# Attention of 2048 queries: V products and row sums of two steps put together, with six slots of probabilities, a K ring of six and a Q ring of three

## The reference, cut to what matters

```python
q, k, v = jnp.split(qkv, 3, axis=-1)
scores = jnp.einsum('bhqd,bhkd->bhqk', q, k) / np.sqrt(HEAD_DIM)
causal = jnp.tril(jnp.ones((S, S), dtype=bool))[None, None]
scores = jnp.where(causal, scores, NEG)
probs = jax.nn.softmax(scores, axis=-1)
ctx = jnp.einsum('bhqk,bhkd->bhqd', probs, v)
return ctx.transpose(0, 2, 1, 3).reshape(B, S, DIM) @ W_out + b_out
```

## Time and profile before

| | |
|---|---|
| median of 3 runs | 2070.89 us (2069.48 to 2071.95) |
| time of the profiled execution | 2070.12 us, its span 2067.9 us |
| PE busy over the span | 1959.5 us (95%) |
| DVE busy | 1076.5 us (52%) |
| ACT busy | 638.3 us (31%) |
| POOL busy | 454.2 us (22%) |
| mean granted clock of TensorE | 0.983 |

### The profile page before, as it was taken

The page is one execution under the profiler, slowest core; times in us unless marked ns, Lnnn a source line. Parts: engine busy times, 40 slices in busy tenths (PEclk is TensorE's granted clock), DMA queues, the critical chain, the costliest instruction groups (busy, mean ns, idle before and its releaser), DMA issues. The chain is left out here.

```text
span 2067.9 us, 25594 instructions
## 1 busy us (share of the span) xinstructions
PE 1959.5 (95%) x10088; PEld 1398.7 (68%) x10088; DVE 1076.5 (52%) x1860; ACT 638.3 (31%) x1152; POOL 454.2 (22%) x401
## 2 busy tenths in 40 slices
PE   6999999999999997889999999997998979999998
PEld 4677555445555545678888888885885668888886
DVE  4456877667666725743434443436434575434334
ACT  3231355446455563422112111113221332111111
POOL 0122766666645266100000000000002110000000
PEclk9999999999999999999999999999999999999999
DMA  8653421422421003200000000002001011000002
GB/s 311 224 161 124 93 52 43 93 53 53 97 46 27 20 1 133 67 31 31 30 2 31 31 31 1 1 1 90 6 6 31 0 41 41 24 28 21 5 1 82
DMA packets 61720, 111.86 MB, mean 54 GB/s; under 512 B 6000, under 2 KB 21248, under 8 KB 61568
## 3 DMA queue, kind: packets, MB, share of 16 engines
q1 hardware_dynamic: 54144, 85.05, 14.3%
q0 software_dynamic: 7456, 25.18, 4.1%
HBM read 84.77 MB, written 25.44 MB: 53 GB/s over the span
## 5 line engine op out<-in xcount | busy, mean ns | idle before, releaser
L450 DVE TENSOR_REDUCE part_max<-banks 128x1 f32<-128x512 f32 (+2 forms) x640 | 357.5, 615 | 154.7 <-PE banks L422 95.0
L921 ACT ACTIVATE probs<-banks 128x512 f32<-128x512 f32 (+3 forms) x640 | 310.7, 538 | 281.1 <-PE banks L848 141.1
L422 PE MATMUL banks<-kst,qst 96*128 96x512 f32 (+2 forms) x640 | 261.4, 417 | 12.9 <-DVE part_max L450 9.2
L844 PE MATMUL banks<-qst,kst 98*128 98x512 f32 (+2 forms) x640 | 250.8, 412 | 0.2 <-ACT probs L921 0.2
L1423 DVE TENSOR_TENSOR tokens_a<-banks,tokens_a 128x512 f32<-128x512 f32 x224 | 151.6, 688 | 69.6 <-PE banks L214 68.9
L212 PE MATMUL banks<-h_hi,f_w_first 128*128 128x512 f32 x448 | 177.3, 396 | 9.5 <-DVE h_lo L199 9.5
L1448 DVE TENSOR_TENSOR tokens_b<-banks,tokens_b 128x512 f32<-128x512 f32 x64 | 44.3, 692 | 270.0 <-ACT tokens_b L1367 270.0
L213 PE MATMUL banks<-h_lo,f_w_first 128*128 128x512 f32 x448 | 176.9, 395 | 0.0
L212 PE MATMUL banks<-f_d_hi,f_hid_hi 128*128 128x512 f32 x432 | 170.0, 393 | 6.7 <-issue 3.6
L214 PE MATMUL banks<-h_hi,f_w_first 128*128 128x512 f32 x448 | 176.3, 393 | 0.0
L213 PE MATMUL banks<-f_d_lo,f_hid_hi 128*128 128x512 f32 x432 | 168.2, 389 | 0.0
(11 more groups left out here) (187 smaller groups left out, 3251.8 us busy)
## 6 DMA issues: line engine op xcount, KB each, us to landing
tokens_a<-in_L_wmod SPq DMA_DIRECT2D x12, 1024.0 KB, 7.9
qst<-q_hi SPq DMA_DIRECT2D x32, 256.0 KB, 6.1
kst<-k_hi SPq DMA_DIRECT2D x32, 256.0 KB, 8.2
x<-in_L_attn_x SPq DMA_DIRECT2D x4, 1024.0 KB, 12.9
q_hi<-qk_out_hi POOLq DMA_DIRECT2D x16, 256.0 KB, 3.0
q_lo<-qk_out_lo POOLq DMA_DIRECT2D x16, 256.0 KB, 3.3
k_hi<-qk_out_hi POOLq DMA_DIRECT2D x16, 256.0 KB, 4.2
k_lo<-qk_out_lo POOLq DMA_DIRECT2D x16, 256.0 KB, 4.3
```

The lines of the kernel that those rows point to most:

```text
L422: mm = nc.tensor.matmul(dst[:, 0:wide], qst[n % QS][0:BIASROW, h, P * t:P * t + P], kst[(NB * g + c) % KS][0:BIASROW, h, 0:wide], start=Tr ...
L450: nc.vector.tensor_reduce(part_max[:, n % 2, ht, c:c + 1], max_bank(slot)[:, 0:wide], AX_X, ALU.max).then_inc(max_read, 1)
L844: mm = nc.tensor.matmul(dst[:, c0:512], kst[ck % KS][0:BIASROW + 2, h, at:at + P], qst[n % QS][0:BIASROW + 2, h, c0:512], start=True, stop ...
L921: nc.scalar.activation(probs[:, q % PS, h, c0:512], score_bank(sh)[:, c0:512], ACT.Exp, scale=SCALE).then_inc(exp_done, 1)
```

## The change

The middle is done once for two steps. Steps s and s+1 (s even, always of one block) form a pair, and TensorE's order is: both quads of step s; then one middle with `sum_pair(s-3)`, `context(s-2)`, `context(s-1)` and `sum_pair(s-2)`; then both quads of step s+1. Probabilities have six slots, because they live longer. To pay for the two slots in SBUF, Q has three buffers instead of four and K six instead of seven. So `load(3)` moves from the start of the attention to the end of block 0's scores, and every later `load(n)` waits for block n-3 instead of n-4; `schedule()` uses the same QS, so its limits move too. For n = 6, 7, 10, 11, 14 and 15 the turn of block n-1 now stands ahead of the first tile of block n. `finalize` moves from the second quad of a block's first step to the first quad of its second step, and waits for `pairs_used` too. The waits of ACT on GpSimd's pair sums go back three steps instead of two.

```diff
-            QS = 4
-            KS = 7
-            PS = 4
+            QS = 3
+            KS = 6
+            PS = 6
...
-                    if n and i == TURN_AFTER:
+                    if n and i == (0 if n % NB in (2, 3) and n > QS else TURN_AFTER):
                         slots.append((n - 1, tiles_of(n - 1)))
...
-                for n in range(3):
+                for n in range(QS):
                     load(n)
                 rows_of_max(0)
-                load(3)
...
                 def sum_pair(s):
                     n, i = steps[s]
+                    if not off_diagonal(s):
+                        return
...
-                for s, (n, i) in enumerate(steps):
+                for s in range(0, len(steps), 2):
                     phase(s, 0)
-                    if s >= 2 and off_diagonal(s - 2):
+                    phase(s, 1)
+                    if s:
+                        if s >= 4:
+                            sum_pair(s - 3)
+                        context(s - 2)
+                        context(s - 1)
                         sum_pair(s - 2)
-                    if s:
-                        context(s - 1)
-                    phase(s, 1)
+                    phase(s + 1, 0)
+                    phase(s + 1, 1)
+                sum_pair(len(steps) - 3)
+                context(len(steps) - 2)
                 context(len(steps) - 1)
...
-                            if q >= PS and off_diagonal(s - 2):
-                                act.wait_ge(pair_ready, 4 * off_index(s - 2) + h + 1)
+                            if q >= PS and off_diagonal(s - 3):
+                                act.wait_ge(pair_ready, 4 * off_index(s - 3) + h + 1)
...
                     if part == 0:
                         dve.wait_ge(probs_read, quads_before(n + 1))
+                        if j:
+                            dve.wait_ge(pairs_used, off_before(n + 1))
...
-                    for slot in max_of_quad[2 * s]:
-                        max_vector(dve, slot)
-                    tiles = max_of_quad[2 * s + 1]
+                    tiles = max_of_quad[2 * s]
                     for part in range(4):
-                        if n and i == 0:
+                        if n and i == 1:
                             finalize(n - 1, part)
                         for slot in tiles[len(tiles) * part // 4:len(tiles) * (part + 1) // 4]:
                             max_vector(dve, slot)
+                    for slot in max_of_quad[2 * s + 1]:
+                        max_vector(dve, slot)
```

## The result

The changed kernel takes **2172.97 us** (2171.31 to 2182.06, four runs) against 2070.18 us before: a ratio of 1.051, 95% interval 1.048 to 1.054, or 103 us more. The direction was forecast, the size wasn't: 2127 us was, with a range that ends at 2158.

A forecast was written before the change was run, and what follows sets the result against it. TensorE was taken to bound the attention, busy 567 of 581 us. Merge -14.4, slots +58, turns +1.5, loads +5 and clock +6 gave +56 us on 2070.9: 2127 us, range 2095 to 2158.

The forecast's parts named there:

- The bursts: Crowded quads with 17, 16 and 16 slots, where VectorE sets the pace: 12.2 us lost three times, 36 us.
- about 5.5: Sign in the attention: 40 middles of about 5.5 us instead of 80 of 2.9.
- 80 us or more: Sign in the attention: TensorE's wait for VectorE's reductions grows from 45 us to 80 or more.
- part 5: Half-clock windows where VectorE is full; middles falling into them take 1.7 us more: +6 us (0 to 35).
- third rival: TensorE stays at 1.2 GHz for most of the bursts, 16 us each, 48 in three: 2169 us, chance 0.10.
- Part 4: Turns right behind their block's last tile, +1.5 us (0 to 5); late Q and K loads, +5 (0 to 24).
- Parts 1 and 2: Merging 80 middles into 40 saves 14.4 us; four quads between middles lengthen stretches set by the slowest engine.
- The rule of three instructions' head start: Stretch between middles takes the longer of TensorE's sum and the slowest engine's quad-by-quad sum less 1.5 us.
- droughts: Quads without maximum tiles, where ScalarE needs 2.0 us against TensorE's 0.94: 9 us in the three groups.
- part 3: Three Q buffers change the slots in each quad: 78 us lost less 20 lost before, +58 us.
- the switch wins: The 40 saved middles, 14.4 us, outweigh VectorE's lag: 2056 us, chance 0.04.
- The middle rival: Crowded quads cost only themselves: 36 us, 6 for empty quads, -14 for merging: 2098 us, chance 0.16.

The follow-up runs named there:

- e5: Kernel before, with its buffers and single middles, given the changed kernel's slots in each quad and places of the turns: 2149.27 us.
- e1: Changed kernel with one middle in each step and finalize in its old place, keeping its buffers and slots: 2167.36 us.
- e7: Changed kernel with single middles and the even slots of the kernel before, products of unloaded blocks using the newest loaded operands: 2082.72 us.
- e6: Changed kernel, middles merged, with the even slots of the kernel before, products of unloaded blocks using the newest loaded operands: 2103.47 us.
- e3: Changed kernel with each maximum product issued twice in quads with more than 8 slots: 2174.53 us.
- e4: Changed kernel with VectorE reducing only 128 columns of each maximum tile in quads with more than 8 slots: 2122.81 us.
- e8: e6 with every maximum reduction cut to 128 columns: 2052.31 us.
- e9: e7 with every maximum reduction cut to 128 columns: 2059.45 us.
- e12: e5 with every maximum reduction cut to 128 columns: 2064.68 us.
- e11: Kernel before with every maximum reduction cut to 128 columns: 2035.56 us.

## Why the prediction was right in its sign and wrong in its size

**The account.** 103 us = 79 (slots, e5 over before) + 18 (buffers, e1 over e5) + 6 (merged middles, changed kernel over e1). The last two depend on the first: with even slots they are 12 and 21 (e7, e6).

**Right.** The bursts were found from `schedule()` ahead of the run, and they are where the loss is. VectorE's price of 0.52 to 0.55 us a tile held (0.55 in e3), and so did that of a burst's lag: 12.2 us forecast, 11.5 at most in block 9 (e3 over e4). The middle of block 15 took 5.29 us against "about 5.5". K came late at the first tile of blocks 6 and 10 (0.60 and 0.78 us), not of 14. The sign "80 us or more" for TensorE's wait for VectorE didn't come: it was 67.

**The step that failed is part 5, the clock: "+6 (0 to 35)".** Half-clock windows were few and short in the kernel before, and I priced them singly, in "a little over half" of six stretches, at 1.7 us each. In the changed kernel the six longest last 14 to 24 us. By the two mean clocks (0.947 of 2171 us, 0.983 of 2068) some 160 us more of the run are at 1.2 GHz, nearly 120 of them in blocks 5, 9 and 13. At block 9's 0.2 us each those cost 24 us; the other 40, at the third of a us of e3's spread or the 0.4 of e4, cost 13 to 17. This makes an estimate of 37 to 41 us for a term that was put at 6, so 31 to 35 of the 46 us that the forecast missed. What I argued was that "while VectorE sets the pace, a slower TensorE costs little". That holds in the crowded quads themselves (19.5 against 18.2 us). But the clock didn't come back when TensorE was full again: it stayed low through middles, empty quads and quads with seven slots behind the burst. My third rival said this and gave 2169 us, within 4 us of the result, and I gave it 0.10. That it came so near is in part luck: it had 16 us for the clock in each burst, and block 9 shows 8.7. For it I had a row of 0.50 behind each VectorE-bound stretch; against it only one stretch of 17 us, with a far lighter lag. The Trainium skill (TensorE: Matmul & The Clock Gate, Part 1) has the low level as the default that sustained activity lifts. The rule agrees with e3, where more products held the clock up, but e4 shows TensorE busy for 20.50 of 20.50 us at the lower level; no run here settles what would have lifted it.

**Part 4, loads and turns: loads "+5 (0 to 24)", measured 12 to 18 with the other buffers.** It was mis-sized and within its bounds. The waits themselves are small (8.4 us in e7); the rest is by my reading the clock that falls behind them, which I had not joined to this term. The turns, "+1.5 (0 to 5)", were too low as well: their weight loads wait 10.4 us in seven places, against 2.6 before.

**Parts 1 and 2, the merge.** The switch was priced right where nothing else binds: 2 x 2.71 - 5.29 = 0.13 us, and 0.23 more at the edges of a run of scores (763.38 to 765.49 less 1.88). But its 14 us were booked as if they came in every pair. e8 and e9 show 7, with VectorE's lag taken out, and block 15 loses 3 us of its own to ScalarE. The rule of three instructions' head start, which I fitted to the kernel before, makes the merge at even slots worth nothing (a loss grown from 20 to 33 us, less the 14); measured was +21. By the same rule the bunched slots with single middles lose 26 us; e5 lost 79. The clock, which the rule doesn't have, is not all of this: with the short reductions (0.29 us a tile) the rule gives about 5 us, and e12 over e11 is 29 with the clock at 0.982 in both. So, by the waits, the rule has the empty quads at ScalarE's pace too cheap; "9 us" of droughts stood in part 3, and the scores' waits for ScalarE grew by 19 us (7 to 26) in the changed kernel.

**The rival of the faster side** ("the switch wins") fell where I said it would be decided: VectorE's lag costs more than 14 us. The middle rival, 2098 us, fails even at full clock: 2173 less the 37 to 41 us of the clock is 2132 or more.

**What stays open.** The 50 us are split into lag and clock by block 9 alone (11.5 and 8.7 us of 20.2), from single executions. No experiment changed the clock and nothing else: e3 was meant to and its median didn't move. How the 29 us divide between empty quads and turns is read from waits, not tried. And what holds the clock down while TensorE is full isn't known.

## What to carry to other kernels

A buffer count that also feeds a planner changes the order of work, and that can be worth far more than the edit it pays for: here 79 us against a possible 14. When engines are balanced, a longer run between two kinds of work needs more buffered slack for every engine that is hidden behind it: without it, merging cost 21 us here, and with a faster VectorE it gained 7. And a stretch in which another engine sets TensorE's pace is to be priced with the clock that it leaves behind, not only with its own waits.

## What the runs showed of the hardware

The granted clock fell behind waits of TensorE for VectorE's banks or for a DMA of 0.6 to 2.8 us, and then stayed at 0.50 for 20.5 us while TensorE was never idle (e4, block 5); behind a wait of 0.4 us in block 9 it didn't fall. Doubling the maximum products kept it at 1.00 through quads 44 and 45 of the profiled run (e3). The same kernel's runs differ by 24 us in step with their mean clocks (e3), so a single run of such a kernel says little. A us at half clock cost about 0.2 us where VectorE set the pace (block 9, changed kernel against e3), and a little over 0.4 where TensorE did (e4, block 5 against 9).
